# One pool of PSUM banks for everything TensorE writes, with softplus on GpSimd, in a decoder layer

## What is computed

```python
x = x + attn(layernorm(x), w_qkv, w_o)            # rotary, 16 heads of 32, causal softmax
x = x + ssm(ctx, z=layernorm(x), ...)             # below
x = x + bitlinear(gelu(bitlinear(layernorm(x), w_fc)), w_proj)

# ssm, per sequence
u = silu(conv4(in_proj @ ctx) + conv_b)
dt_lo, Bm, Cm = split(x_proj @ u)                 # 16, 16, 16 rows
delta = softplus(dt_proj @ dt_lo + dt_b)
state = state * exp(delta * A) + (delta * u) * Bm # 16 states, scan over 512 tokens
y = (sum_n state_n * Cm_n + D * u) * silu(z)

# bitlinear: layer norm, scale by the row's largest magnitude, product with sign(round(w / mean|w|)) * mean|w|
```

## Time and profile before

| | |
|---|---|
| runs, median (lowest to highest) | 1259.14 us (1258.46 to 1260.72) |
| profiled execution, its own time | 1260.95 us |
| its span in the trace | 1259.2 us |
| TensorE busy | 1023.9 us (81%) |
| VectorE busy | 1033.9 us (82%) |
| ScalarE busy | 836.5 us (66%) |
| GpSimd busy | 558.7 us (44%) |

### The profile page before, as it was taken

One profiled execution on the slowest core, in us unless ns is written; L12 is line 12 of the kernel. 1 busy time (PEld: TensorE's weight loads), 2 busy tenths in 40 slices (PEclk: granted clock), 3 DMA queues, 4 the chain that ended last, 5 costly groups with the idle time before them and its releaser, 6 DMA issues.

```text
span 1259.2 us, 17217 instructions
## 1 busy us (share of the span) xinstructions
PE 1023.9 (81%) x5268; PEld 751.1 (60%) x5268; DVE 1033.9 (82%) x1399; ACT 836.5 (66%) x1577; POOL 558.7 (44%) x462
## 2 busy tenths in 40 slices
PE   5877887799678989789989756665789889879897
PEld 2234654468545566655658545554567667668776
DVE  5668787875899988799987879978999999997744
ACT  4753665564787775687885876681997878863332
POOL 1346523551446551356641413439646565552401
PEclk9778969899799987899989768787799999999998
DMA  5216632444324552324452252161001110100000
GB/s 191 83 37 185 175 93 92 126 146 131 92 82 137 176 167 62 105 75 153 151 186 74 69 199 69 52 234 46 18 30 35 46 33 23 30 14 9 17 18 17
DMA packets 59353, 115.80 MB, mean 92 GB/s; under 512 B 8880, under 2 KB 13232, under 8 KB 58240
## 3 DMA queue, kind: packets, MB, share of 16 engines
q1 hardware_dynamic: 59264, 114.70, 29.2%
HBM read 90.42 MB, written 24.25 MB: 91 GB/s over the span
## 4 chain that ended last, share of the span: by engine, by line
PE 42%; DVE 31%; ACT 10%; issue 9%; POOL 4%; DMA 1%; SPq 1%; DVEq 0%; ACTq 0%; POOLq 0%
PE ps L1670 6%; DVE hb L1773 6%; PE ps L1600 6%; PE ps L1753 5%; DVE y_acc L1795 5%; PE ps L1640 5%; PE ps L1743 4%; PE ps L1683 3%; PE ps L1614 3%; DVE du L1825 3%; DVE m_col L1870 2%; PE ps L1626 2%; ACT ps L1329 2%; PE ps L1653 2%; DVE fh L1999 2%
## 5 line engine op out<-in xcount | busy, mean ns | idle before, releaser
L1216 POOL TENSOR_TENSOR hb<-du,b_bc 128x1024 f32<-128x1024 f32 (+1 forms) x160 | 311.1, 1966 | 260.7 <-PE ps L1670 260.6
L1773 DVE TENSOR_TENSOR_SCAN hb<-ps,hb 128x1024 f32<-128x1024 f32 (+1 forms) x128 | 257.1, 2012 | 30.9 <-ACT ps L1329 22.3
L1329 ACT ACTIVATE ps<-delta,a_neg 128x511 f32<-128x511 f32 (+2 forms) x320 | 179.8, 597 | 72.5 <-DVE hb L1773 62.4
L1670 PE MATMUL ps<-ident,hb 128*128 128x128 f32 x1088 | 180.1, 305 | 58.8 <-DVE hb L1773 26.0
L1795 DVE SCALAR_TENSOR_TENSOR y_acc<-ps,ct,y_acc 128x512 f32<-128x512 f32 x256 | 183.4, 741 | 34.1 <-PE ps L1670 32.6
L1670 PEld LDWEIGHTS ps<-ident,hb 128*128 128x128 f32 x1088 | 139.2, 158 | 87.1 <-issue 43.8
L1443 ACT ACTIVATE p_q<-ps,m_col 128x512 f32<-128x512 f32 (+3 forms) x256 | 132.0, 523 | 50.2 <-DVE m_col L1870 43.8
L1640 PE MATMUL ps<-ident,p_q 128*128 128x128 f32 x640 | 107.0, 314 | 38.1 <-ACT p_q L1443 29.6
L1626 PE MATMUL ps<-k_st,q_st 128*128 128x512 f32 (+3 forms) x256 | 99.3, 431 | 36.8 <-ACT p_q L1443 24.3
L1460 ACT ACTIVATE p_t<-ps 128x512 f32<-128x512 f32 x160 | 89.8, 595 | 55.8 <-PE ps L1640 55.4
L1600 PE MATMUL ps<-xn_t,w_ring 128*128 128x512 f32 x256 | 119.2, 609 | 6.7 <-DVE tmp L1853 5.5
(11 more groups left out here) (148 smaller groups left out, 2037.7 us busy)
## 6 DMA issues: line engine op xcount, KB each, us to landing
w_ring<-in_w_attn SPq DMA_DIRECT2D x32, 512.0 KB, 3.8
qk_d<-hl SPq DMA_DIRECT2D x64, 256.0 KB
q_st<-qk_d SPq DMA_DIRECT2D x128, 128.0 KB, 2.8
b_bc<-bc_d SPq DMA_DIRECT2D x48, 256.0 KB, 3.4
k_st<-qk_d SPq DMA_DIRECT2D x64, 128.0 KB, 2.7
k_st<-qk_d SPq DMA_DIRECT2D x128, 64.0 KB, 2.3
x_in<-in_x SPq DMA_DIRECT2D x16, 256.0 KB, 3.3
raw_fc<-in_w_fc SPq DMA_DIRECT2D x4, 1024.0 KB, 8.0
```

The lines of the kernel that those rows point to most:

```text
L1216: nc.gpsimd.tensor_tensor(piece_of(e, hi, lo).rearrange("p (a n) -> p a n", a=2), du[b % 2][:, 2 * h:2 * h + 2, lo:hi], b_bc[:, i % BC_RIN ...
L1329: ins = nc.scalar.activation(factors(j, hi, lo)[:, (hi - lo) * m + start:(hi - lo) * (m + 1)], delta[b % 2][:, et, lo + start:hi], ACT.Exp ...
L1670: mm = nc.tensor.transpose(Y[q % 2][:, P * et:P * et + P], piece_of(2 * r + et // 2, hi, lo)[:, at:at + P], ident[:])
L1773: v.tensor_tensor_scan(h, d, h, 0.0, ALU.mult, ALU.add).then_inc(scan_done, 1)
```

## The change

The rings become one pool: an item that TensorE writes takes, of all eight banks (4 and 5 only after the last scan), the one whose last user is estimated to be done first. `plan()` notes the bank and its last user in PLACE, and the kernel waits for that user alone. TensorE may now run the scores of a slot before the transposes of the slot before. From batch 1 on, GpSimd does the four instructions of delta. ScalarE writes max(value, 0) at once (Relu) and takes the magnitude from the bank. The tables of due times have a set for each batch, and many of their numbers and weights differ.

```diff
-STATE = {'exp': [-3, 3], 'dbu': [-19.1, -14.1], 'scan': [0, 6], 'ht': [7.6, 8.8, 10, 11.2]}
+STATE = {'exp': [-3, 3], 'dbu': [-19.1, -2.9], 'scan': [0, 6], 'ht': [7.6, 8.8, 10, 11.2]}
...
+DA_BANKS = (4, 5)
+def delta_by(b):
+    return "pool" if b else "dve"
...
     elif kind == "delta":
         b, et = a
-        yield "dve", 3, [act("dt", *a)] + ([act("exp", 2 * DS * (b - 1) - 1), pool("du", b - 2, et)] if b >= 2 else [])
+        if b == 0:
+            yield "dve", 3, [act("dt", *a)]
+        else:
+            yield "pool", 6, [act("dt", *a)] + ([act("exp", 2 * DS * (b - 1) - 1), pool("du", b - 2, et)] if b >= 2 else [])
...
     elif kind == "s":
         p, n = a
-        r = 10 * p + n
-        yield "pe", 0.62, [sp("stack", p)] + ([act("e", p, n - 2) if n >= 2 else act("t", p - 1, n + 3)] if r >= 2 else [])
-        yield "dve", 0.8, [pe(*item)]
+        yield "pe", 0.62, [sp("stack", p)]
+        yield "dve", 0.8, [pe(*item)] + ([act("e", p - 1, n)] if p else [])
     elif kind == "e":
-        yield "act", 1.3, [dve("s", *a)]
+        yield "act", 1.3, [dve("s", *a)] + ([pe("t", a[0] - 1, 4)] if a[0] else [])
...
-    held = [[("dve", ("wo", B - 1, 1, 1))], [("dve", ("wo", B - 1, 1, 1))], [("act", ("t", SLOTS - 1, 4))],
-            [("act", ("t", SLOTS - 1, 4))], [("dve", ("scan", PIECES - 1))], [("dve", ("scan", PIECES - 1))]]
+    held = [[("dve", ("scan", PIECES - 1))] if n in DA_BANKS else [] for n in range(8)]
...
     def bank():
-        return min(((over[users[-1]], n) for n, users in enumerate(held) if users[-1] in over), default=None)
+        return min(((over[users[-1]] if users else 0.0, n) for n, users in enumerate(held) if not users or users[-1] in over),
+                   default=None)
...
-            users = taken[name]
-            if len(users) >= 2:
-                if users[-2] not in over:
-                    return None
-                at = max(at, over[users[-2]])
+        if (engine, item) in last_use:
+            if not bank():
+                return None
+            at = max(at, bank()[0])
...
-            for p in range(SLOTS):
-                assert at["s", p, 4] < at["t", p, 0] and (p == 0 or at["t", p - 1, 4] < at["s", p, 0])
...
-        M = [ps[:, 0, :], ps[:, 1, :]]
-        R = [ps[:, 2, :], ps[:, 3, :]]
-        da = ps[:, 4:6, :]
-        Y = [ps[:, 6, :], ps[:, 7, :]]
-        F = [ps[:, n, :] for n in range(6)]
+        da = ps[:, DA_BANKS[0]:DA_BANKS[-1] + 1, :]
...
+        def bank(*item):
+            return ps[:, PLACE[item][0], :]
...
+        def bank_free(*item):
+            if PLACE[item][1] is None:
+                return
+            _, user = PLACE[item][1]
             kind, *a = user
+            if user in TASK:
+                emptied(nc.tensor, TASK[user])
+            elif user in Y_TURN:
+                y_taken(nc.tensor, user)
+            elif kind == "e":
+                nc.tensor.wait_ge(e_done, 5 * a[0] + a[1] + 1)
             elif kind == "t":
-                nc.tensor.wait_ge(p_ready, 5 * SLOTS)
+                nc.tensor.wait_ge(p_ready, 5 * a[0] + a[1] + 1)
...
+                elif kind == "delta":
+                    b, et = a
+                    pool.wait_ge(sp_ready, ET * b + et + 1)
+                    if b >= 2:
+                        pool.wait_ge(da_ready, 2 * DS * (b - 1))
+                    d = delta[b % 2][:, et, :]
+                    own.done(nc.gpsimd.tensor_scalar(d, tmp[:, 1, :], 1.0, 1.0, ALU.add, ALU.subtract))
+                    own.settle()
+                    own.done(nc.gpsimd.tensor_tensor(d, tmp[:, 1, :], d, ALU.subtract))
+                    own.settle()
+                    own.done(nc.gpsimd.tensor_tensor(d, d, tmp[:, 2, :], ALU.add))
+                    own.settle()
+                    nc.gpsimd.tensor_tensor(d, d, tmp[:, 0, :], ALU.add).then_inc(delta_ready["pool"], 1)
...
-                    nc.scalar.activation(tmp[:, 0, :], M[n % 2], ACT.Identity, bias=dt_b[:, et, :])\
+                    nc.scalar.activation(tmp[:, 0, :], bank(kind, *a), ACT.Relu, bias=dt_b[:, et, :])
+                    nc.scalar.activation(tmp[:, 1, :], bank(kind, *a), ACT.Abs, bias=dt_b[:, et, :])\
                         .then_inc(m_free["act"], 1)
                     act.wait_ge(m_free["act"], FREED[n][1])
-                    own.done(nc.scalar.activation(tmp[:, 1, :], tmp[:, 0, :], ACT.Abs))
-                    own.settle()
...
+                    if p:
+                        act.wait_ge(t_full, 5 * p)
...
+                    if p:
+                        dve.wait_ge(e_done, 5 * (p - 1) + n + 1)
...
+                    if t >= 4:
+                        pool.wait_ge(gelu_done, 4 * (t - 3))
```

More of the change, by code:

```diff
@@ L155 @@
          'hn': 0},
- 'dve': {'scan': -2,
+ 'dve': {'scan': -1.9,
          'ht': 0,
-         'ln1a': 0,
-         'ln1b': 0,
-         'inproj': 1.5,
+         'ln1a': 0.1,
+         'ln1b': 7.7,
+         'inproj': 1.3,
          'delta': 0,
-         'rot': 0,
+         'rot': 12.2,
          's': -0.5,
@@ L672, in plan @@
             over[engine, item] = at + us + 0.2
-        if (engine, item) in ring:
-            name, user = ring[engine, item]
-            if name == "f":
-                held[bank()[1]].append(user)
-                if item[0] in ("xt", "ht_ffn"):
-                    for who in ("act", "dve") if turns else ():
-                        before[who, item] = before[who, item] + [(who, turns[-1])]
-                    turns.append(item)
-            else:
-                taken[name].append(user)
+        if (engine, item) in last_use:
+            n = bank()[1]
+            place[item] = n, held[n][-1] if held[n] else None
+            held[n].append(last_use[engine, item])
+            if item[0] in ("xt", "ht_ffn"):
+                for who in ("act", "dve") if turns else ():
+                    before[who, item] = before[who, item] + [(who, turns[-1])]
+                turns.append(item)
         if engine == "pe" and (item[0] == "dt" or item[0] == "rot" and item[3] == 0):
-            scratch.append(("dve", ("delta", *item[1:])) if item[0] == "dt" else ("pool", ("lo", *item[1:3])))
-    return out, held
-ORDER, HELD = plan()
+            scratch.append((delta_by(item[1]), ("delta", *item[1:])) if item[0] == "dt" else ("pool", ("lo", *item[1:3])))
+    return out, place
+ORDER, PLACE = plan()
 ORDER["pe"] = [x for item in ORDER["pe"] for x in ((("first", item), item) if item[0] in W_KINDS else (item,))]
@@ L1360, in _ @@
                         act.wait_ge(xadd_done, LT * (b - 1))
-                    nc.scalar.activation(y_acc[:, b % 2, tb, :], y_bank((kind, r, tb)), ACT.Copy).then_inc(y_free["act"], 1)
+                    nc.scalar.activation(y_acc[:, b % 2, tb, :], bank(kind, r, tb), ACT.Copy).then_inc(y_free["act"], 1)
                 elif kind == "ln1b":
@@ L1473, in _ @@
                     act.wait_ge(m_full, n + 1)
-                    nc.scalar.activation(o_t[:, g % 4, :], M[n % 2], ACT.Copy).then_inc(m_free["act"], 1)
+                    nc.scalar.activation(o_t[:, g % 4, :], bank(kind, *a), ACT.Copy).then_inc(m_free["act"], 1)
                 elif kind == "gate":
@@ L1499, in _ @@
                     act.wait_ge(tr_full, tr + 1)
[L1500 removed]
+                    nc.scalar.activation(dst, bank(kind, *a).rearrange("p (k n) -> p k n", n=P), ACT.Copy)\
                         .then_inc(tr_hi, 1)
@@ L1609, in _ @@
                     emptied(pe, TASK["ln1b", b, LT - 1])
-                    freed(pe, n)
+                    bank_free(kind, *a)
                     m = 0 if first else 1
@@ L1794, in _ @@
                     y = y_acc[:, b % 2, tb, :]
-                    v.scalar_tensor_tensor(out=y, in0=y_bank((kind, r, tb)), scalar=ct[:, b % 2, tb, n:n + 1], in1=y,
+                    v.scalar_tensor_tensor(out=y, in0=bank(kind, r, tb), scalar=ct[:, b % 2, tb, n:n + 1], in1=y,
                                            op0=ALU.mult, op1=ALU.add).then_inc(y_free["dve"], 1)
@@ L1847, in _ @@
                     task = TASK[(kind, *a)]
-                    bank = M[task % 2]
+                    src = bank(kind, *a)
                     consts(dve, "rotary")
@@ L1983, in _ @@
                     dve.wait_ge(tr_hi, tr + 1)
-                    v.scalar_tensor_tensor(out=dst, in0=F[BANK[(kind, *a)]].rearrange("p (k n) -> p k n", n=P), scalar=-1.0,
+                    v.scalar_tensor_tensor(out=dst, in0=bank(kind, *a).rearrange("p (k n) -> p k n", n=P), scalar=-1.0,
                                            in1=hi.bitcast(F32), op0=ALU.max, op1=ALU.subtract).then_inc(tr_free, 1)
@@ L2018, in _ @@
                         dve.wait_ge(y_stored[t % 2], 16 * (t // 2))
-                    v.scalar_tensor_tensor(out=y_out[:, t % 2, :], in0=F[BANK[kind, t]], scalar=fh[:, t % 4, 12:13],
+                    v.scalar_tensor_tensor(out=y_out[:, t % 2, :], in0=bank(kind, t), scalar=fh[:, t % 4, 12:13],
```

380 lines of the change are left out of this document (201 added, 179 removed), and 3 rows, old and new, of the table ATTN_END.

## The result

Four runs of the changed kernel took 1186.67 us in the median (1185.84 to 1188.71), against 1258.8 us for the kernel before on the same chip: a ratio of 0.9428, 95% interval 0.9411 to 0.9446. I forecast 1225 us and gave 1200 as the lower end. The gain is 72 us, twice what I booked, and the range misses it by 13. The profiled execution took 1185.84 us, with a span of 1184.0 us.

A forecast was written before the change was run, and what follows sets the result against it. No engine was full from 115 to 875 us; VectorE bound 875 to 1135, TensorE the end. Stage gains 8 + 7 + 7 + 16, minus 3 behind attention, made 35 us less: 1225 us, range 1200 to 1260.

The forecast's parts named there:

- the slower rival: VectorE's scans wait for GpSimd's products around the deltas of batches 1 to 3: up to 1294 us; chance 0.11.
- The bank waits of the earlier trace: TensorE, 115 to 875 us: 67.4 us of waits for one of two banks, the most the pool can give back.
- I take the densest stage as what TensorE can hold: 88%: Attention stages to 692 us: TensorE's work over 0.88, the share of 512 to 692 us, gives the first two lengths.
- All four stages by their own limits: Attention, 115 to 875 us: three stages bound by TensorE, the last by VectorE; 8, 7, 7 and 16 us less.
- STATE, the second product: GpSimd's second product of a state comes 11.2 due units later, thinning the cover that hides the deltas; cost booked at nothing.
- the softplus in the last stage alone (16 us): 692 to 875 us: VectorE, rid of 9.98 us of softplus, at 86.7% busy takes 167 us, 16 us less.
- An overlap saves only the step from score to maximum; it lies inside the 67.4 us: Slot boundaries, 15 of 31 overlapping: next exponentials still wait for all transposes, so no gain beyond the bank waits.
- The time freed is filled by other waits: Attention stages: only 692 to 875 us gains, half its 16 us: 1251 us; 3 to 15 us less, chance 0.15.
- All bank waits go: Attention stages: no data wait follows the bank waits, 64 us less, 1196 us; chance 0.14 for over 45 us less.
- The shared reads decide: VectorE's 24 convolutions all stretch to 2.85 us beside GpSimd: 36 us come back, 1259 us; chance 0.03.
- My 3 us more: VectorE's convolutions, 115 to 875 us: GpSimd's added SBUF reads stretch them by 3 us, within the TensorE-bound stages.
- The rule of the Trainium skill that I cited: SBUF: VectorE's two-port or two-SBUF-input operations and GpSimd's take shared ports exclusively for a whole instruction; the loser blocks.

The follow-up runs named there:

- the filled kernels: The changed kernel with bank 7 unused (1272.6 us), plus 385 or 791 idle TensorE products in its gaps: 1267.5 and 1262.7 us.
- slots_apart: The changed kernel, but a slot's scores run only after all transposes of the slot before: 1212.3 us, 0.961 of the kernel before.

## Why the prediction was wrong

**What held.** The gain is in the attention part, and the part behind it kept its length (385.4 us, forecast 384 + 3). A delta takes 5.7 us on GpSimd (forecast 5.8), scans don't wait for it (6.2 us), and the slower rival is out. The bank waits of the earlier trace rows fell from 67.4 us to 20.3, but 15 us of new ones came (L1687 and L1701 after y_acc, L1650 after p_q), so about half is gone, as I took it.

**The step that failed: "I take the densest stage as what TensorE can hold: 88%", over work sums held fixed.** The second step that failed, the tables put at nothing, is below. The cap was nearly right, at 91, 91 and 87% in the first three stages. Over 110 us to the end of attention the share rose from 81.3% (621.65 of 764.4) to 85.3% (587.32 of 688.6). With the old work sum that share gives 621.65/0.853 = 729 us, 36 less; the forecast had 38 there. The other 40 us lie in the numerator: 34 us of work over 0.853. This is arithmetic on the two traces, and no cause by itself. Two things that I held fixed are not. Products after waits ran at 1.2 GHz in the kernel before (0.50 from 161 to 176 us), so waits removed shorten work as well; the filled kernels show this, and also that shorter products alone bring little time. And the busy time of a product that stops before a gap counts its whole latency, 273 ns for a transpose, where eight in a row take 1.04 us, 110 ns from one to the next:

```profile
198.08 1.04 PE L1701 MATMUL ps<-ident,p_q 128*128 128x128 f32 x8
```

So fewer stops make a smaller sum. A busy sum divided by a share was no floor of the stage.

**"All four stages by their own limits."** The 8, 7, 7 and 16 us came out as 11, 43, -5 and 26.5. TensorE did 923 matmuls in the first stage where it had done 849, and 902 in the second where it had 960. In the last, VectorE's share was 85.7% (forecast 86.7%), but it had 134 us of work left and not 145. Work was moved earlier, so the new stages don't hold the same work as the old ones.

**The tables were never booked.** I looked at them for the one thing that could hurt (STATE, the second product). They are worth 17 us of loss with rings and 20 to 26 us of gain with the pool. This is the larger part of the miss: without them the kernel took 1212.2 us, 13 below the forecast and inside the range; with them 1186.7. I had no reason for the nothing. Numbers fitted to another kernel's order are worth nothing, or less, in this one.

**Gains added up that depend on each other.** I booked the softplus in the last stage alone (16 us), as if VectorE's time counted only where it is the bound. With rings that is about right (9 us). With the pool it is worth 31 to 48. "An overlap saves only the step from score to maximum; it lies inside the 67.4 us" is refuted by slots_apart: the wait of transposes for exponentials, which I had called data and left out of the 67.4, goes from 8.9 back to 22.3 us.

**The rivals.** "The time freed is filled by other waits" is what happens to the softplus alone, with rings. "All bank waits go", at 1196 us, had the place of the gain right and its bound wrong: 67.4 us was no bound. Its condition wasn't met either, since about half of such waits are still there. "The shared reads decide": the 24 convolutions in the attention part took 26.8 us, mean 1118 ns, with GpSimd busy 69 us more there, against 32.8 and 1368. My 3 us more came out as 6 less. The rule of the Trainium skill that I cited may well hold for an instruction that collides: four of the eight tiles' three convolutions still took 4.1 to 4.8 us in the changed kernel, where the other four took 2.3. Why there were fewer such in sum, no run separates.

## What to carry to other kernels

Price a change of buffers and a change of load together, since time freed on one engine is used only if the waits of the others can close up behind it; neither alone shows what the pair is worth. When waits go, expect the work itself to shrink where the engine's clock follows its activity, and don't use busy sums at a fixed share as a floor. Numbers that set an order are part of the kernel they were fitted to; compare structures at more than one setting of them, here 1187 to 1213 us for one structure. A variant that loses no more than such a shift has no price of its own yet.
